# A mixture-of-experts phase on one core: expert weights fetched as two transfers of 256-byte runs, one matmul a tile for each product

## The reference

```python
logits = x @ router_w.T + expert_bias          # 8192 tokens, 160 experts
top_w, top_idx = top_k(sigmoid(logits), 8)     # normalized, times 2.5
h1 = silu(einsum('th,eih->eti', x, w_gate))    # H = 128 -> I = 64
routed = einsum('eti,ehi->th', h1 * combine, w_down)   # 64 -> 128
```

## Time and profile before

| | |
|---|---|
| median of three runs | 3749.31 us |
| the profiled execution, its own time | 3751.92 us |
| its span (first to last instruction) | 3750.4 us |
| expert phase, by SP's first and last issue | 1725.5 to 2271.8 us |
| busy share of the span: PE, DVE, ACT, POOL | 66%, 79%, 67%, 63% |
| expert phase, 1800 to 2200 us: granted TensorE clock, DMA share, GB/s | 1.00, 0.81, 243 |

### The profile page before, as it was taken

How to read it: one execution, slowest core, us unless ns; L and a number is a source line. 1 busy time by engine, 2 the same in 40 slices (tenths; PEclk the granted TensorE clock), 3 DMA queues, 4 the chain that set the end, 5 groups by cost and what they waited for, 6 DMA issues and landing times. The chain is left out here.

```text
span 3750.4 us, 64048 instructions
## 1 busy us (share of the span) xinstructions
PE 2475.8 (66%) x21034; PEld 1190.2 (32%) x21034; DVE 2978.3 (79%) x4334; ACT 2500.3 (67%) x1684; POOL 2345.8 (63%) x1620
## 2 busy tenths in 40 slices
PE   4661556666766767667888885566666666666666
PEld 2441112222222222235767662122222222222224
DVE  5886899999898999941433336999999999999991
ACT  1110788888888888862333335878888788777883
POOL 1220888687787878752434446776767777767771
PEclk9896888888888888876999998878787778777875
DMA  7884122222222222225888883123222222222222
GB/s 249 307 305 144 62 70 82 69 83 81 101 85 77 76 81 84 99 66 157 249 241 244 243 243 106 53 73 97 75 79 81 69 83 77 74 75 81 79 68 87
DMA packets 376226, 445.79 MB, mean 119 GB/s; under 512 B 49186, under 2 KB 291698, under 8 KB 376051
## 3 DMA queue, kind: packets, MB, share of 16 engines
q1 hardware_dynamic: 293106, 283.77, 24.1%
q0 software_dynamic: 58752, 148.46, 12.0%
q10 hardware_dynamic: 24192, 11.02, 1.1%
HBM read 239.08 MB, written 204.02 MB: 118 GB/s over the span
## 5 line engine op out<-in xcount | busy, mean ns | idle before, releaser
L1082 DVE SCALAR_TENSOR_TENSOR u_dve<-s_win,rpos,ps_here 128x512 f32<-128x512 f32 x1792 | 1197.5, 740 | 119.6 <-PE ps_l L1174 84.4
L1174 PE MATMUL ps_l<-u_dve,wsel 128*32 128x512 f32 x6144 | 955.9, 751 | 425.4 <-ACT u_dve L991 187.0
L942 POOL TENSOR_TENSOR u_pool<-s_win 128x4096 f32<-128x4096 f32 x128 | 1022.3, 7987 | 7.7 <-DMA s_win<-s_dram 5.2
L993 ACT ACTIVATE u_dve<-u_dve 128x4096 f32<-128x4096 f32 x224 | 809.9, 3616 | 54.5 <-DVE u_dve L1082 54.5
L1077 DVE TENSOR_TENSOR u_dve<-s_win,ps_here 128x4096 f32<-128x4096 f32 x160 | 703.4, 4412 | 35.9 <-PE ps_l L1174 35.8
L930 POOL DMA_INDIRECT yg<-yslot_dram,slot_now x512 | 487.0, 951 | 284.5 <-issue 147.9
L921 POOL DMA_INDIRECT xslot_dram<-xr,slot_now x512 | 498.6, 974 | 147.0 <-issue 143.6
L991 ACT ACTIVATE u_pool<-u_pool,bdmg_sb 128x4096 f32<-128x4096 f32 x128 | 474.4, 3706 | 64.1 <-POOL u_pool L942 64.1
L991 ACT ACTIVATE u_dve<-u_dve,bdmg_sb 128x4096 f32<-128x4096 f32 x128 | 474.4, 3706 | 23.9 <-DVE u_dve L1077 22.2
L1174 PEld LDWEIGHTS ps_l<-u_dve,wsel 128*32 128x32 f32 x6144 | 190.4, 126 | 858.6 <-issue 545.9
L1013 ACT ACTIVATE at_sb<-ps_u 128x512 f32<-128x512 f32 x256 | 151.2, 591 | 362.5 <-PE ps_u L1230 291.4
(11 more groups left out here) (143 smaller groups left out, 3049.3 us busy)
## 6 DMA issues: line engine op xcount, KB each, us to landing
band<-band_dram SPq DMA_DIRECT2D x32, 2048.0 KB, 7.9
xslot_dram<-zero SPq DMA_DIRECT2D x16, 2688.0 KB, 10.0
xs<-xslot_dram SPq DMA_DIRECT2D x168, 256.0 KB, 3.7
yslot_dram<-ys POOLq DMA_DIRECT2D x168, 256.0 KB, 3.3
band_dram<-ml SPq DMA_DIRECT2D x64, 512.0 KB, 5.2
we<-in_w_expert SPq DMA_DIRECT2D x336, 64.0 KB, 2.8
s_win<-s_dram SPq DMA_DIRECT2D x64, 288.0 KB, 5.8
s_dram<-s_sb POOLq DMA_DIRECT2D x16, 1024.0 KB, 4.7
```

The lines of the kernel that those rows point to most:

```text
L942: pool.tensor_tensor(item_buffer(n), windows(par, ty, d0, 8), s_win[:, par, ty, PAD:PAD + TC].unsqueeze(1).to_broadcast([P, 8, TC]), ALU.s ...
L993: act.activation(u, u, ACT.Gelu).then_inc(gelu_done, 1)
L1082: last = dve.scalar_tensor_tensor(out=item_buffer(n)[:, d, :], in0=s_win[:, par, ty, d0 + d + 1:d0 + d + 1 + TC], scalar=rpos[:, d0 + d:d0 ...
L1174: last = pe.matmul(ps_l[32 * g:32 * g + 32, cgrp % 2, ty, :], wsel[:, ty, q, :], item_buffer(n)[:, d, :], start=(q == 0), stop=(q == 3))
```

## The change

The weights of a tile are now two transfers. `wu` takes columns 0 to 63 of the 128 rows: 128 runs of 256 bytes, to 128 partitions. `wdn` takes columns 64 to 127: rows 0 to 63 and 64 to 127 side by side, 2 runs of 256 bytes on each of 64 partitions, on partitions 0 to 63 for tiles 0 and 2, and on 64 to 127 for tiles 1 and 3. An even tile's hidden values are now on partitions 0 to 63 only, and an odd tile's on 64 to 127 only. So `up` is one matmul a tile, the sigmoid and the product work on 128 x 256 elements, and `down` is one matmul a tile, with 128 output columns. The copy of the result moves as many elements as before, with the tiles in another order in PSUM. The bytes moved are the same. Waits stand where they stood, with doubled counts for the weights.

```diff
-            we = sb("we", [P, BUF, TB, P], F32, c)
+            wu = sb("wu", [P, BUF, TB, I], F32, c)
+            wdn = sb("wdn", [P, BUF, TB // 2, C], F32, c)
...
-            sg = sb("sg", [P, 2, TB * P], F32, c)
-            hs = sb("hs", [P, 2, TB * P], F32, c)
+            sg = sb("sg", [P, 2, TB * P // 2], F32, c)
+            hs = sb("hs", [P, 2, TB * P // 2], F32, c)
...
                         row = e.value_load(te_sb[0:1, bass.ds(n * TB + i, 1)], min_val=0, max_val=NE - 1)
-                        e.dma_start(we[:, u, i, :], w_expert[bass.ds(row, 1)].rearrange("e p f -> p (e f)"))\
+                        part = slice(i % 2 * I, i % 2 * I + I)
+                        e.dma_start(wu[:, u, i, :], w_expert[bass.ds(row, 1), :, 0:I].rearrange("e p f -> p (e f)"))\
+                            .then_inc(loaded_by[u], 16)
+                        e.dma_start(wdn[part, u, i // 2, :].rearrange("p (h f) -> p h f", h=2),
+                                    w_expert[bass.ds(row, 1), :, I:2 * I].rearrange("e (h p) f -> p (e h) f", h=2))\
                             .then_inc(loaded_by[u], 16)
...
-                            for half in range(2):
-                                last = pe.matmul(ps_e[half * I:(half + 1) * I, u % 2, i * P:(i + 1) * P],
-                                                 we[:, u, i, 0:I], xsT[:, u % 2, i * P:(i + 1) * P],
-                                                 start=True, stop=True)
+                            last = pe.matmul(ps_e[i % 2 * I:i % 2 * I + I, u % 2, i // 2 * P:i // 2 * P + P],
+                                             wu[:, u, i, :], xsT[:, u % 2, i * P:(i + 1) * P], start=True, stop=True)
...
-                            for half in range(2):
-                                rows = slice(half * I, (half + 1) * I)
-                                last = pe.matmul(ps_z[:, u % 2, half, i * I:(i + 1) * I],
-                                                 hs[rows, u % 2, i * P:(i + 1) * P], we[rows, u, i, I:2 * I],
-                                                 start=True, stop=True)
+                            part = slice(i % 2 * I, i % 2 * I + I)
+                            last = pe.matmul(ps_z[:, u % 2, i % 2, i // 2 * P:i // 2 * P + P],
+                                             hs[part, u % 2, i // 2 * P:i // 2 * P + P], wdn[part, u, i // 2, :],
+                                             start=True, stop=True)
...
-                        act.activation(sg[:, u % 2], ps_e[:, u % 2], ACT.Sigmoid).then_inc(gate_done, 1)
+                        act.activation(sg[:, u % 2], ps_e[:, u % 2, 0:TB * P // 2], ACT.Sigmoid).then_inc(gate_done, 1)
```

More of the change, by code:

```diff
@@ L1245, in moe_attention_layer @@
             xs = sb("xs", [P, BUF, TB, C], F32, c)
-            we = sb("we", [P, BUF, TB, P], F32, c)
+            wu = sb("wu", [P, BUF, TB, I], F32, c)
+            wdn = sb("wdn", [P, BUF, TB // 2, C], F32, c)
             xsT = sb("xsT", [P, 2, TB * P], F32, c)
-            sg = sb("sg", [P, 2, TB * P], F32, c)
-            hs = sb("hs", [P, 2, TB * P], F32, c)
+            sg = sb("sg", [P, 2, TB * P // 2], F32, c)
+            hs = sb("hs", [P, 2, TB * P // 2], F32, c)
             ys = sb("ys", [P, BUF, TB, C], F32, c)
             ps_x = c.enter_context(nc.psum_tensor("ps_x", [P, 2, TB * P], F32))
-            ps_e = c.enter_context(nc.psum_tensor("ps_e", [P, 2, TB * P], F32))
+            ps_e = c.enter_context(nc.psum_tensor("ps_e", [P, 2, 512], F32))
             ps_z = c.enter_context(nc.psum_tensor("ps_z", [P, 2, 2, 512], F32))
@@ L1316, in up @@
                     def up(n, k, u):
-                        pe.wait_ge(experts_loaded[u], 16 * (TB - 1) * (k + 1))
-                        pe.wait_ge(experts_loaded_pool[u], 16 * (k + 1))
+                        pe.wait_ge(experts_loaded[u], 32 * (TB - 1) * (k + 1))
+                        pe.wait_ge(experts_loaded_pool[u], 32 * (k + 1))
                         pe.wait_ge(rows_copied, n + 1)
@@ L1374, in hidden @@
                             dve.wait_ge(down_done, n - 1)
-                        dve.tensor_tensor(hs[:, u % 2], sg[:, u % 2], ps_e[:, u % 2], ALU.mult).then_inc(hidden_done, 1)
+                        dve.tensor_tensor(hs[:, u % 2], sg[:, u % 2], ps_e[:, u % 2, 0:TB * P // 2], ALU.mult)\
+                            .then_inc(hidden_done, 1)
                     def copy_out(n, k, u):
@@ L1380, in copy_out @@
                             dve.wait_ge(ys_stored[u], 16 * k)
-                        dve.tensor_copy(ys[:, u].rearrange("p i (h c) -> p h i c", h=2),
-                                        ps_z[:, u % 2, :, 0:TB * I].rearrange("p h (i c) -> p h i c", i=TB))\
+                        dve.tensor_copy(ys[:, u].rearrange("p (q b) c -> p b q c", b=2),
+                                        ps_z[:, u % 2, :, 0:TB * I].rearrange("p b (q c) -> p b q c", q=TB // 2))\
                             .then_inc(ys_ready, 1)
```

## The result

The changed kernel takes 4014.33 us, the median of 4 runs (4012.3 to 4020.14), beside 3750.61 us for the kernel before; the ratio is 1.0704, with a 95% interval of 1.0685 to 1.0723. Slower, as forecast, and 109 us beyond the forecast of 3905 us, 34 us outside the range. The profiled execution took 4020.14 us, its span is 4018.6.

The account below looks back on a forecast made before the run. It took SP's instruction stream as the bound: 0.94 us more a batch over 167 batches gives 3751.9 + 157 − 1 = 3907.9 us, and with the profiled execution 2.6 us above the median, 3905 us; range 3845 to 3980.

Parts of the forecast that it names:

- SP is the bound: Expert phase: SP's own instructions, 3.11 us a loop, set the pace of 3.246 us a batch.
- occasional stall: SP's loop in the expert phase: 0.14 us a batch beyond its instructions, which could go (−23 us) or double (+23 us).
- SP, two more transfers a batch: SP's loop: 0.47 us for each added transfer (0.40 to 0.55), 0.94 us a batch, +157 us over 167 batches.
- ACT and POOL, one more each: Weight loads on ACT and POOL: one more transfer each stays under the 4.19 us pace, worth 0.
- PE: Expert phase matmuls: work falls to 1.6 to 2.15 us a batch, worth 0 mid-phase; −1 to −2 us in the drain.
- The clock: TensorE in the expert phase: often at 1.2 GHz, 3.1 to 4.1 us a batch, taken as 0, up to +50 us.
- DMA engines: Expert phase transfers: 47.5 to 56.5 engine-us a batch, 71 to 84% of the 4.19 us pace, worth 0.
- statement on short transfers: Weight transfers: line rate wants at least 512 bytes; the prediction set against it 1.37 times the time per byte at 256.
- the scaling with the transfers' work: Rival, expert phase: pace follows the DMA engines' work, 3.67 us, +71 us, 3820; chance 0.12, shared with cheaper issues.
- the dear packets: Rival, weight transfers: short packets cost as much as long ones, +186 us, 3934 (0.12), or double, 4091 or more (0.05).
- PE at the lower clock: Rival, expert phase: PE at 1.2 GHz becomes the bound, 4.5 us a batch, +209 us, 3957; chance 0.07.
- The not-slower case: Rival: SP is held back inside its loop, so added issues hide; pace 2.97 us, −46 us, 3703; chance 0.04.

Follow-up runs that it names:

- e5: Kernel before with the rows' transfer (`xs`) issued by ACT in place of SP: 3683.4 us, ratio 0.9836 to the kernel before.
- e8: Changed kernel with the rows' transfer (`xs`) issued by ACT in place of SP: 3920.9 us, ratio 1.0471 to the kernel before.
- e2: Kernel before, compute untouched, each tile's weights fetched as two plain transfers of 256-byte runs to 128 partitions: 3935.0 us, ratio 1.0504.
- e10: Kernel before with all its transfers but the changed kernel's lighter compute, routed output not right: 3758.8 us, ratio 1.0026.
- e1: Changed kernel with a tile's two transfers swapped, `wdn` ahead of `wu`: 4063.1 us, one run.
- e4: Changed kernel's compute with one transfer a tile, 128 runs of 768 bytes, down weights on both partition halves: 3767.1 us, ratio 1.0057 to the kernel before.

## Why the prediction was wrong, step by step

- *SP is the bound*: right. e5 and e8 show it from one side, e2 from the other, and e10 that the lighter compute was worth nothing. Of the "occasional stall" of 0.14 us, 0.09 were late table reads. It neither went nor doubled: the pace is now 4.829 − 4.72 = 0.11 us above the loop.
- *SP, two more transfers a batch*: the step that failed, by its size. I took 0.47 us each, bounded by 0.40 and 0.55. A plain one costs 0.52 from issue to issue (e2's pace gives (4.343 − 3.246) / 2 = 0.55, with 0.03 of it later table reads), and the form of `wdn` 0.28 more; by the pace the two make 1.583 / 2 = 0.79, far above my upper end. Twice 0.32 us over 167 batches is 107 us, nearly the whole miss of 109. The smaller part of it, 0.05 us a transfer, is the base: the row of 0.467 is of transfers with a fixed address, each of 0.43 us with one gap and no register instruction, where the added one has 0.333 + 0.037 + 0.029 us and three gaps of about 0.04. (Read from issue to issue that row is 0.475 us, as the last of the six has no gap behind it.) The larger part, 0.28 us, is the form. I had priced `wdn`'s third dimension by `xs`, and had not priced its 64 partitions at all, though the trace of before has that row: in the first microseconds, the one transfer to 64 partitions.

```profile
6.34 0.43 SPq L166 DMA_DIRECT2D wgs_sb<-in_w_gate_sharedT  x1
6.81 0.58 SPq L166 DMA_DIRECT2D wds_sb<-in_w_down_sharedT  x1
7.43 0.58 SPq L166 DMA_DIRECT2D wc_sb<-in_w_cproj  x1
8.05 0.43 SPq L166 DMA_DIRECT2D bias_sb<-in_expert_bias  x1
```

  `wc_sb`, a plain one to 128 partitions, pays behind it, as `wu` does in e1. The upper bound should have come from this row: 0.58 + 0.04 + 0.03 and three gaps, some 0.76 us.
- *ACT and POOL, one more each*: right, worth 0; PE's wait is for SP's `xs` in every batch.
- *PE*: right that it waits. It does so for 1.72 us a batch rather than 2 or more, as at 1.2 GHz its work on a batch takes 3.3 us and not the 1.6 to 2.15 of the full clock.
- *The clock*: right in kind (0.57 on average) and in price; PE's 3.3 us stay below SP's 4.72.
- *DMA engines*: right that they don't bind, but their work was put too high: 44.6 engine-us a batch, below the 47.5 to 56.5 forecast, as a short packet took 16.6 ns and not 18.9 or more. Of the statement on short transfers in the Trainium skill (DMA: Bandwidth & Descriptors, Specifications), the runs show a weak form at most: 256 bytes take 0.62 of the time of 512 here, 1.25 times as much a byte, not twice. Its remark that initiating a transfer is usually small beside the transfer (the same page, "Issuing engines are not separate DMA queues") is borne out for one transfer: `wu` is issued in 0.34 us and lands 2.1 us from its issue (the row below: size, median to landing, 1850 to 2450 us). But landings overlap and the issues of one queue don't, so in this loop it is the issues that add up, and another issuer for one transfer saved 63 us (e5).

```profile
wu<-in_w_expert SPq DMA_DIRECT2D x249, 32.0 KB, 2.1
```

- *The rivals*: the scaling with the transfers' work, the dear packets and PE at the lower clock (3.3 us a batch where 4.5 was feared) are refuted by the share of 0.57 with PE waiting for `xs`. The not-slower case is refuted by the result. Its idea of a table read that is late was true in part, for 0.09 us a batch before.

## What to carry to other kernels

When a queue issues in a loop and the consumer waits for what it issues as it lands, with buffers to spare, count that queue's instructions as one would an engine's: each plain small transfer costs about half a microsecond there, and its bytes hardly matter (0.333 us of issue for 64 KB before and for 32 KB in e2, and for 96 KB in e4). Price an added transfer by a row of the same form (partitions and pieces), not by its neighbours; where the trace has none, the range must reach to the dearest form it has. Before halving the compute, look at whether the consumer waits at all; here moving one transfer to another queue gave 63 us, and halving the products gave none.

## What the runs showed of the hardware that I had not expected

- The issue of a transfer costs by form: on SP, 0.32 to 0.37 us for a plain one to 16, 32, 96 or 128 partitions, 0.49 to 0.54 for a plain one to 64, and 0.55 to 0.64 for forms of two short pieces a partition.
- A slow form makes a transfer right behind it dearer: 0.454 against 0.338 us for `wu` in e1, 0.60 against 0.44 for `xs`.
- POOL's issue of the same `wdn` took 0.606 us against 0.547 for `wu`: the form matters far less there.
- With the lighter compute SP's table reads are late more often, though nothing of SP's was changed (mean 0.363 against 0.318 us, pace 3.306 against 3.246).
